# Recommendation tower: sixteen tables by one-hot matmul instead of fourteen, 64 gathers instead of 72, and one-hot rows widened from 16-bit rows

## Chip, core and metric

One core of one Trainium2 chip. The metric is the time of the whole program on the device, in microseconds (us), median of the runs shown.

## What is computed

512 samples each pick one row of 128 numbers from each of 32 tables (11 tables of 1,000 rows, 12 of 1,250, eight of 12,500, one of 125,000). Every pair of the 32 picked rows is multiplied out (496 dot products per sample), and a three-layer network runs on them:

```python
e = jnp.stack([tbl_0[ids[:, 0]], tbl_1[ids[:, 1]], ..., tbl_31[ids[:, 31]]], axis=1)
dot = jnp.einsum('bnd,bmd->bnm', e, e)
z = dot[:, iu, ju]                                  # 496 pairs, iu < ju
h = jnp.concatenate([z, dense_ctx], axis=1)         # 16 more columns
h = jnp.maximum(h @ W_top1 + b_top1, 0.0)           # 512 -> 512
h = jnp.maximum(h @ W_top2 + b_top2, 0.0)           # 512 -> 256
y = h @ W_top3                                      # 256 -> 1
```

All of it is fp32.

## The kernel before

The program is written engine by engine; each engine runs its list in order, and semaphores hold the lists together. It has two stages.

**Stage 1, picks and gathers.** Rows come into `emb` (128 partitions = the 128 numbers of a row, then sample, then table) in two ways.

A *pick* serves one small table (the 14 smallest, `PICK`). The table is loaded whole, cut in `KR` chunks of 128 rows (8 chunks for 1,000 rows, 10 for 1,250). For each chunk a one-hot row block `onehot` (128 x 512: is this row the one that sample wants?) is made, and TensorE multiplies the chunk by it (L562, L564). Since fp32r keeps only part of an fp32 number, the chunk is split in `high` (a rounded copy, ScalarE, L413) and `low` (what is left, VectorE, L310), and each chunk is two matmuls of 512 columns into `two_ps`. `onehot` is a ring of 16 chunks (`HOT`), tables and their halves are held threefold. VectorE makes most one-hot chunks by comparing ids with row numbers (L327, three chunks at a time; L317, one at a time, in the first two picks). ScalarE makes `BY_ACT` chunks of each pick (34 of the 118) in two passes per chunk: `away` = |id - row| (L420), then 1 - that, cut at zero (L435). `pick_out` copies two finished picks from `two_ps` to `emb`, `pick_alone` one (the last two).

A *gather* serves the other 18 tables: GpSimd issues an indirect DMA that fetches 128 rows (L301), 72 in all, in 20 banks. Of each block of 128 samples, one bank has 2 gathers of one table each (`lone0`, `lone1`, `MORE` = 2), and four banks have 4 (`TB`), each of 32 samples x 4 tables. TensorE turns a bank (`turn`, 2 or 4 transposes into `turn_ps`), ScalarE copies it to `emb` (`emb_out`). `rows` holds four banks (`ROWS_HELD`), so the gathers of bank k wait until bank k-4 was turned. In stage 1, TensorE turns bank t-1 behind pick t.

In stage 1, ScalarE's list per pick t is: one-hot chunks of pick t+2, `pick_out` at odd t, `emb_out(t-1)`, `away` of pick t+3, `high` of pick t+3. VectorE's is: `low` of a piece, one-hot chunks, `low` of the next piece, and so on.

**Stage 2, dots and layers.** TensorE forms the dot products of 64 samples at a time (`dot_group`, 2 x 32 small matmuls, L604), in two pairs of PSUM banks by turns; ScalarE and VectorE copy one half each to `dot_sb` (`dots_out`), the four 32-row parts go to HBM and come back skewed as `pairs` (`half_out`, `half_in` on ScalarE's queue, `block_out`, `block_in` on SyncE's), and layer 1 (L623), layer 2 (L634) and layer 3 (L639) follow. TensorE's list: `dot_group` 0 to 3, turn of bank 14, `dot_group` 4 and 5, turns of banks 15 and 16, the first half of group 6, layer 1 of blocks 0 and 1, turns of banks 17 and 18, and so on to the last bank, which is turned and multiplied in two halves among layer 1 of block 2.

Of the kernel before, what the change touches and what calls it, by code (L numbers as in the profile page):

```python
# [4 lines left out]
P = 128  # L5
# [5 lines left out]
PICK = 14  # L11
# [24 lines left out]
BY_ACT = [2, 1, 2, 2, 2, 2, 2, 2, 3, 2, 2, 4, 4, 4]  # L36
# [34 lines left out]
def build(nc, row_ids, pick_ids, tables, lone0, lone1, picked, context, w1, w2, small, y):  # L71
# [4 lines left out]
    with ctx:  # L76
# [9 lines left out]
        lone = [lone0, lone1]  # L86
        ident = sb("ident", [P, P], f32)
        id_sb = sb("id_sb", [P, 2, TILE0[NB]], i32)
        row_no = sb("row_no", [P, TILE0[NB]], i32)
# [4 lines left out]
        own_row = sb("own_row", [P, KR[0]], f32)  # L94
        less_row = sb("less_row", [P, len(STEPS), KRMAX], f32)
# [7 lines left out]
        away = sb("away", [P, AWAY, B], mybir.dt.float16)  # L103
# [48 lines left out]
        less_row_ready = sem("less_row_ready")  # L152
# [4 lines left out]
        away_ready = sem("away_ready")  # L157
# [68 lines left out]
        def _(sp):  # L226
            def ids_load(t):
                if t >= IDS_HELD:
                    sp.wait_ge(onehot_dve, by_dve(t - IDS_HELD + 1))
                    sp.wait_ge(away_ready, ACT0[t - IDS_HELD + 1])  # L230
                sp.dma_start(pick_id[:, t % IDS_HELD, :], pick_ids[:, t, :]).then_inc(pick_ids_in[t], 16)
# [53 lines left out]
        def _(pool):  # L285
# [6 lines left out]
            pool.wait_ge(row_ids_in, 16)  # L292
            for k in range(NB):
                if k == 1:
                    pool.wait_ge(row_no_ready, 1)
                if k >= ROWS_HELD:
                    pool.wait_ge(turned, k - ROWS_HELD + 1)
                for i in range(TILES[k]):
                    c = TILE0[k] + i
                    one_table = k % BANKS == 0  # L300
                    pool.indirect_dma_start(  # L301
                        rows[:, k % ROWS_HELD, i, :], None, lone[i] if one_table else tables,
                        bass.IndirectOffsetOnAxis(ap=id_sb[:, 0, c:c + 1] if one_table else row_no[:, c:c + 1], axis=0)
# [3 lines left out]
        def _(dve):  # L307
# [5 lines left out]
            def make_onehots(t, k0, k1):  # L313

                i, k = STEPS.index(KR[t]), k0
                while t < ALONE and k < k1:
                    dve.tensor_scalar(onehot[:, CHUNK0[t] + k, :], pick_id[:, t, :], own_row[:, k:k + 1], None,  # L317
                                      ALU.is_equal).then_inc(onehot_dve, 1)
                    k += 1
                while k < k1:  # L320
# [7 lines left out]
                    k += n  # L328

# [12 lines left out]
            dve.tensor_copy(own_row[:, :], own_row_i[:, 0, 0:KR[0]]).then_inc(own_row_ready, 1)  # L342
            dve.wait_ge(row_ids_in, 16)
            dve.tensor_tensor(row_no[:, :], id_sb[:, 0, :], id_sb[:, 1, :].bitcast(f32), ALU.add).then_inc(row_no_ready, 1)
            dve.wait_ge(own_row_ready, len(STEPS) + 1)
            for i, k in enumerate(STEPS):
                dve.tensor_scalar(less_row[:, i, 0:k], own_ps[:, i, 0:k], -1.0, None, ALU.mult).then_inc(less_row_ready, 1)
# [53 lines left out]
        def _(act):  # L401
# [371 lines left out]
```

## Time and profile before

| | |
|---|---|
| median of 3 runs | 121.43 us (121.08 to 122.03) |
| span of the profiled execution | 149.4 us |
| TensorE matmul busy | 118.9 us (80%) |
| VectorE busy | 76.3 us (51%) |
| ScalarE busy | 79.4 us (53%) |
| GpSimd busy | 72.0 us (48%) |
| mean granted TensorE clock | 0.931 |
| HBM read, written | 17.02 MB, 2.13 MB |

The profiled execution is 28 us longer than the median run. Busy time is the sum of an engine's instructions; shares are of the span and mix both stages. Times in the trace count from the span's start.

### The profile page before, as it was taken

How to read it: one execution, taken by the hardware profiler on the slowest of the kernel's cores; microseconds unless marked ns; L12 is line 12 of the kernel's file. 1: busy time of each engine (PE TensorE's matmuls, PEld its weight loads, DVE VectorE, ACT ScalarE, POOL GpSimd, SP SyncE). 2: the span in 40 equal slices, each digit the busy share in tenths (PEclk: the TensorE clock that was granted, in tenths of full speed). 3: DMA queues.
4: the chain of work that ended last, by engine and by line, in shares of the span. 5: the costliest groups of instructions: out<-in, count | busy, mean ns of one | idle time of the engine just before them, and what ended most of it. 6: DMA issues, size and time to landing. Idle time of an engine off the chain costs nothing.

```text
span 149.4 us, 2614 instructions
## 1 busy us (share of the span) xinstructions
PE 118.9 (80%) x1008; PEld 95.5 (64%) x1008; DVE 76.3 (51%) x106; ACT 79.4 (53%) x128; POOL 72.0 (48%) x80
## 2 busy tenths in 40 slices
PE   0689993599996998798799931289829899999994
PEld 0568871268773875486566721289729788998972
DVE  2999961199969996984969000013103033123411
ACT  3699674199939969999999300030512112210022
POOL 3787777278747747747747777300550720000000
PEclk9999999569999999999999996559986999999999
DMA  4798763136763587379511121102471731015000
GB/s 136 248 335 306 234 207 97 35 61 212 225 205 81 190 263 239 72 241 311 170 35 47 50 55 50 47 0 72 136 222 35 202 77 41 7 35 171 9 0 1
DMA packets 10990, 19.29 MB, mean 129 GB/s; under 512 B 2385, under 2 KB 7377, under 8 KB 10978
## 3 DMA queue, kind: packets, MB, share of 16 engines
q1 hardware_dynamic: 7234, 12.96, 27.9%
q0 software_dynamic: 2304, 4.72, 11.7%
q10 hardware_dynamic: 1440, 1.44, 2.8%
q8 instruction: 8, 0.13, 0.4%
q14 instruction: 4, 0.03, 0.1%
HBM read 17.02 MB, written 2.13 MB: 128 GB/s over the span
## 4 chain that ended last, share of the span: by engine, by line
PE 66%; issue 15%; DVE 11%; ACT 4%; DMA 2%; DVEq 1%; SPq 0%
PE two_ps L562 16%; PE two_ps L564 14%; DVE onehot L327 8%; PE free_ps L604 8%; PE two_ps L623 8%; PE two_ps L604 7%; PE turn_ps L572 4%; DVE low L310 3%; PE free_ps L634 3%; PE two_ps L634 2%; ACT emb L403 2%; DMA home<-picked 2%; PE two_ps L639 1%; PE turn_ps L623 1%; DVEq L364 1%
## 5 line engine op out<-in xcount | busy, mean ns | idle before, releaser
L301 POOL DMA_INDIRECT rows<-tables,row_no x64 | 63.4, 991 | 39.4 <-issue 18.0
L562 PE MATMUL two_ps<-onehot,high 128*128 128x512 f32 x118 | 50.9, 432 | 12.6 <-DVE low L310 5.2
L564 PE MATMUL two_ps<-onehot,low 128*128 128x512 f32 x118 | 48.2, 408 | 1.3 <-issue 1.3
L327 DVE TENSOR_TENSOR onehot<-pick_id,free_ps 128x1536 fp32r<-128x1536 int16 (+2 forms) x25 | 41.5, 1662 | 6.4 <-remote 5.2
L562 PEld LDWEIGHTS two_ps<-onehot,high 128*128 128x128 f32 x118 | 23.4, 198 | 23.7 <-issue 15.1
L564 PEld LDWEIGHTS two_ps<-onehot,low 128*128 128x128 f32 x118 | 23.6, 200 | 5.5 <-issue 1.5
L310 DVE TENSOR_TENSOR low<-home,high 128x512 fp32r<-128x512 f32 (+1 forms) x33 | 20.8, 631 | 8.6 <-issue 6.3
L420 ACT ACTIVATE away<-pick_id,less_row 128x512 f16<-128x512 int16 x34 | 22.3, 712 | 0.0
L604 PE MATMUL free_ps<-emb 128*64 128x64 f32 x272 | 12.7, 231 | 11.8 <-issue 10.5
L435 ACT ACTIVATE onehot<-away 128x512 fp32r<-128x512 f16 x34 | 19.2, 622 | 2.0 <-remote 1.9
L604 PEld LDWEIGHTS free_ps<-emb 128*64 128x64 f32 x272 | 10.7, 140 | 14.0 <-issue 11.9
L403 ACT ACTIVATE emb<-turn_ps 128x512 f32<-128x512 f32 (+1 forms) x20 | 10.8, 545 | 15.3 <-PE turn_ps L572 6.9
L403 ACT ACTIVATE high<-home 128x1024 fp32r<-128x1024 f32 (+2 forms) x17 | 15.9, 937 | 2.0 <-DMA home<-picked 2.0
L192 DVE COPY home<-free_ps 128x512 f32<-128x512 f32 x4 | 2.8, 692 | 24.3 <-PE free_ps L604 24.3
L403 ACT ACTIVATE home<-free_ps 128x512 f32<-128x512 f32 (+1 forms) x5 | 2.8, 554 | 22.6 <-remote 19.7
L623 PE MATMUL two_ps<-pairs,w_sb 128*128 128x128 f32 x104 | 12.9, 278 | 0.3 <-issue 0.3
L623 PEld LDWEIGHTS two_ps<-pairs,w_sb 128*128 128x128 f32 x104 | 12.1, 192 | 0.7 <-issue 0.5
L403 ACT ACTIVATE emb<-two_ps 128x1024 f32<-128x1024 f32 (+1 forms) x8 | 8.9, 1117 | 6.2 <-PE two_ps L564 6.2
L572 PE MATMUL turn_ps<-ident,rows 128*128 128x128 f32 x68 | 11.0, 283 | 1.4 <-issue 1.4
L604 PE MATMUL two_ps<-emb 128*64 128x64 f32 x240 | 10.9, 265 | 1.1 <-issue 1.1
L301 POOL DMA_INDIRECT rows<-lone,id_sb x8 | 7.7, 968 | 8.1 <-remote 2.9
L331 DVE TENSOR_SCALAR h<-two_ps,small_sb 128x128 f32<-128x128 f32 x15 | 4.3, 345 | 13.8 <-PE two_ps L623 12.9
(38 smaller groups left out, 63.2 us busy)
## 6 DMA issues: line engine op xcount, KB each, us to landing
home<-picked SPq DMA_DIRECT2D x10, 512.0 KB
home<-picked SPq DMA_DIRECT2D x3, 640.0 KB
pick_id<-pick_ids SPq DMA_DIRECT2D x12, 128.0 KB
w_sb<-w SPq DMA_DIRECT2D x3, 512.0 KB
dot_out<-home SPq DMA_DIRECT2D x10, 128.0 KB, 2.3
rows<-tables,row_no POOLq DMA_INDIRECT x64
dot_out<-home ACTq DMA_DIRECT2D x6, 128.0 KB, 2.5
pairs<-dot_out SPq DMA_DIRECT2D x10, 64.0 KB, 2.0
```

What stands on the lines that cost most here:

```text
L301: pool.indirect_dma_start(rows[:, k % ROWS_HELD, i, :], None, lone[i] if one_table else tables, bass.IndirectOffsetOnAxis(ap=id_sb[:, 0, c ...
L310: dve.tensor_tensor(low[:, at, a:b], table[:, at, a:b], high[:, at, a:b], ALU.subtract).then_inc(low_ready, 1)
L327: dve.tensor_tensor(onehot[:, c % HOT:c % HOT + n, :], ids, own, ALU.is_equal).then_inc(onehot_dve, n)
L403: return act.activation(out, in_, ACT.Copy)
L420: act.activation(away[:, m % AWAY, :], pick_id[:, t % IDS_HELD, :], ACT.Abs, bias=less_row[:, i, k:k + 1]).then_inc(away_ready, 1)
L435: act.activation(onehot[:, c % HOT, :], away[:, m % AWAY, :], ACT.Relu, bias=1.0, scale=-1.0).then_inc(onehot_act, 1)
L562: pe.matmul(out, high[:, at, D * k:D * (k + 1)], onehot[:, c % HOT, :], start=(k == 0), stop=False)
L564: pe.matmul(out, low[:, at, D * k:D * (k + 1)], onehot[:, c % HOT, :], start=False, stop=(k == KR[t] - 1)).then_inc(picked_done, 1)
L572: last = pe.transpose(turn_ps[k % 2][:, i * P:(i + 1) * P], rows[:, k % ROWS_HELD, i, :], ident[:, :])
L604: last = pe.matmul(out, e, e, start=True, stop=True, tile_position=(0, 64 * h))
L623: last = pe.matmul(h1_ps[r][n], w1_sb[:, c, n * P:(n + 1) * P], pairs[:, r:r + 1, :, c, :], start=(c == 0), stop=(c == PC - 1))
L634: return pe.matmul(h2_ps[part][n], w2_sb[:, c, n * P:(n + 1) * P], h1[:, c, samples(part)], start=(c == 0), stop=(c == N1 - 1))
```

## The change

- `PICK` 14 to 16: two tables of 1,250 rows more are picked, 138 chunks instead of 118. The order of the first fourteen picks stays.
- The gathers lose the two `lone` tables: 64 gathers, 16 equal banks of four, all of 32 samples x 4 tables.
- `LAG` = 3: TensorE turns bank t-3 behind pick t (before: bank t-1), and ScalarE's `emb_out` follows with the same lag. Banks 0 to 12 are turned in stage 1, so `dot_group` 0 to 5 run without a turn between them; banks 13, 14 and 15 are turned where 17, 18 and 19 were.
- ScalarE's `away` passes are gone, and its one-hot chunks (`BY_ACT`, now 81 of the 138) are made in two steps on two engines: VectorE compares 16-bit ids with the row number and writes a 16-bit row (`make_narrow`, one instruction per chunk, into `narrow`, two picks held), and ScalarE copies all chunks of a pick to `onehot` at once, 16 bits to fp32r (one instruction, two where the ring wraps).
- VectorE's own one-hot chunks go from 84 to 57. `make_narrow(t+1)` stands ahead of the `low` pieces of pick t.

```diff
-PICK = 14
+PICK = 16
-BY_ACT = [2, 1, 2, 2, 2, 2, 2, 2, 3, 2, 2, 4, 4, 4]
+BY_ACT = [2, 4, 5, 5, 5, 5, 5, 5, 5, 5, 5, 6, 6, 6, 6, 6]
-MORE = GF - 4 * TB
-BANKS = 1 + BLK // SUB
+BANKS = BLK // SUB
-TURNED = PICK - 1
-TABLES_HELD, IDS_HELD, HOT, AWAY, ROWS_HELD = 3, 4, 16, 8, 4
+LAG = 3
+TABLES_HELD, IDS_HELD, HOT, ROWS_HELD = 3, 4, 16, 4
...
+            def make_narrow(t):
+
+                i = STEPS.index(KR[t])
+                if t >= 2:
+                    dve.wait_ge(onehot_act, ACT0[t - 1])
+                for n in range(BY_ACT[t]):
+                    k = ACT_K0[t] + n
+                    dve.tensor_scalar(narrow[:, t % 2, n, :], pick_id[:, t % IDS_HELD, :], own_row[:, i, k:k + 1], None,
+                                      ALU.is_equal).then_inc(narrow_ready, 1)
...
             for j in range(PIECES0):
                 make_onehots(0, PIECE * j, min(PIECE * (j + 1), KR[0] - BY_ACT[0]))
+                if j == 1:
+                    make_narrow(0)
                 if j == PIECES0 - 1:
                     dve.wait_ge(pick_ids_in[1], 16)
+                    make_narrow(1)
                     make_onehots(1, DVE_K0[1], DVE_K0[1] + AHEAD)
...
             for t in range(1, PICK):
+                if t + 1 < PICK:
+                    dve.wait_ge(pick_ids_in[t + 1], 16)
+                    make_narrow(t + 1)
                 dve.wait_ge(pick_ids_in[t], 16)
...
             def make_onehots(t):
 
-                for m in range(ACT0[t], ACT0[t + 1]):
-                    c = CHUNK0[t] + ACT_K0[t] - ACT0[t] + m
-                    act.wait_ge(away_ready, m + 1)
-                    if c >= HOT:
-                        act.wait_ge(picked_done, c - HOT + 1)
-                    act.activation(onehot[:, c % HOT, :], away[:, m % AWAY, :], ACT.Relu, bias=1.0, scale=-1.0
-                                   ).then_inc(onehot_act, 1)
+                act.wait_ge(narrow_ready, ACT0[t + 1])
+                c0, n0 = CHUNK0[t] + ACT_K0[t], 0
+                while n0 < BY_ACT[t]:
+                    at = (c0 + n0) % HOT
+                    n = min(BY_ACT[t] - n0, HOT - at)
+                    if c0 + n0 + n > HOT:
+                        act.wait_ge(picked_done, c0 + n0 + n - HOT)
+                    act.activation(onehot[:, at:at + n, :], narrow[:, t % 2, n0:n0 + n, :], ACT.Copy).then_inc(onehot_act, n)
+                    n0 += n
...
-                if t:
-                    emb_out(t - 1)
+                if t >= LAG:
+                    emb_out(t - LAG)
                 if t + 3 < PICK:
-                    make_away(t + 3)
                     split_high(t + 3)
...
             for t in range(PICK):
                 pick(t)
-                if t:
-                    turn(t - 1)
-            turn(TURNED)
+                if t >= LAG:
+                    turn(t - LAG)
             pe.wait_ge(pick_emb_ready, TWOS + 1)
-            dot_group(0)
-            dot_group(1)
-            dot_group(2)
-            dot_group(3)
-            for k in range(TURNED + 1, NB - 5):
-                turn(k)
-            dot_group(4)
-            dot_group(5)
-            turn(NB - 5)
-            turn(NB - 4)
+            for grp in range(GROUPS - 2):
+                dot_group(grp)
             dot(6, 0)
             pe.wait_ge(weights_in, 64)
             layer1(0)
```

VectorE's list at the start of stage 1, from the third piece of pick 0 (its one-hot chunks) to the first `low` piece of pick 2. Before:

```order
L317 TENSOR_SCALAR onehot<-pick_id,own_row 128x512 x2
L310 TENSOR_TENSOR low<-home,high 128x256
L317 TENSOR_SCALAR onehot<-pick_id,own_row 128x512 x3
L310 TENSOR_TENSOR low<-home,high 128x512
L317 TENSOR_SCALAR onehot<-pick_id,own_row 128x512 x2
L310 TENSOR_TENSOR low<-home,high 128x512 x2
```

And of the change, the same place and the whole list of pick 2 behind it:

```order
L330 TENSOR_SCALAR narrow<-pick_id,own_row 128x512 x4
L310 TENSOR_SCALAR onehot<-pick_id,own_row 128x512 x2
L303 TENSOR_TENSOR low<-home,high 128x256
L330 TENSOR_SCALAR narrow<-pick_id,own_row 128x512 x5
L310 TENSOR_SCALAR onehot<-pick_id,own_row 128x512 x2
L303 TENSOR_TENSOR low<-home,high 128x512 x2
L330 TENSOR_SCALAR narrow<-pick_id,own_row 128x512 x5
L303 TENSOR_TENSOR low<-home,high 128x512
L320 TENSOR_TENSOR onehot<-pick_id,free_ps 128x1536
L303 TENSOR_TENSOR low<-home,high 128x512
```

The last `low` piece of pick 0 and the first of pick 1 now stand behind four and five `narrow` rows; a pick in mid-stage has five `narrow`, two `low` and one three-chunk one-hot, where it had two `low` and two three-chunk one-hots.

ScalarE's list in mid-stage, its part at pick 5 and the first row of the next (with the semaphores it waits for): one-hot chunks of pick 7, picks 4 and 5 out, a bank out, and the work on pick 8. Before:

```order
L435 ACTIVATE onehot<-away 128x512 [waits picked_done,away_ready] x2
L403 ACTIVATE emb<-two_ps 128x512x2 [waits picked_done]
L403 ACTIVATE emb<-turn_ps 128x4x32x4 [waits turned]
L420 ACTIVATE away<-pick_id,less_row 128x512 [waits onehot_act,pick_ids_in8]
L420 ACTIVATE away<-pick_id,less_row 128x512 [waits onehot_act] x2
L403 ACTIVATE high<-home 128x1024 [waits picked_done,table_in8]
L435 ACTIVATE onehot<-away 128x512 [waits picked_done,away_ready] x3
```

And of the change:

```order
L432 ACTIVATE onehot<-narrow 128x2560 [waits picked_done,narrow_ready]
L411 ACTIVATE emb<-two_ps 128x512x2 [waits picked_done]
L411 ACTIVATE emb<-turn_ps 128x4x32x4 [waits turned]
L411 ACTIVATE high<-home 128x1024 [waits picked_done,table_in8]
L432 ACTIVATE onehot<-narrow 128x2560 [waits picked_done,narrow_ready]
```

Two or three one-chunk passes of each of two kinds per pick became one wide copy of five chunks (six in the picks of ten chunks).

TensorE's list at the start of stage 2. Before:

```order
L604 MATMUL two_ps<-emb 64x64 x32
L572 MATMUL turn_ps<-ident,rows 128x128 x4
L604 MATMUL free_ps<-emb 64x64 x32
L604 MATMUL two_ps<-emb 64x64 x32
L572 MATMUL turn_ps<-ident,rows 128x128 x6
L604 MATMUL free_ps<-emb 64x64 x16
L623 MATMUL two_ps<-pairs,w_sb 128x128 x32
```

And of the change:

```order
L581 MATMUL two_ps<-emb 64x64 x32
L581 MATMUL free_ps<-emb 64x64 x32
L581 MATMUL two_ps<-emb 64x64 x32
L581 MATMUL free_ps<-emb 64x64 x16
L600 MATMUL two_ps<-pairs,w_sb 128x128 x32
```

Ten transposes left this place; the dots and layer 1 follow one another.

## Rows read from the trace of the kernel before

**Rows 1.** Core list: span and mean granted TensorE clock.

```profile
core 0: 149.4 us, clock 0.931
```

**Rows 2.** Busy time by stretch: PE, PEld, DVE, ACT, POOL, granted clock, DMA share, GB/s.

```profile
25.00:30.00 5.00, 2.63 (x7) 1.56 (x8) 0.61 (x1) 1.12 (x2) 1.81 (x3) 0.58 0.16 39
```

**Rows 3.** Chain that ended last, stage 2: start, length, what.

```profile
84.83 1.27 PE free_ps L604 x36
...
98.12 3.18 PE two_ps L604 x64
101.31 1.87 PE free_ps L604 x64
...
105.04 0.59 PE turn_ps L572 x4
...
111.64 3.40 PE two_ps L604 x63
115.04 0.82 PE turn_ps L572 x6
...
115.88 0.61 ACT emb L403
```

**Rows 4.** Timeline, 15 to 20 us: start, length, engine, instruction, idle time before it.

```profile
15.03 0.48 PE L562 MATMUL two_ps<-onehot,high 128*128 128x512 f32 x1
...
19.17 0.48 PE L562 MATMUL two_ps<-onehot,high 128*128 128x512 f32 x1
...
19.37 1.14 ACT L403 ACTIVATE emb<-two_ps 128x1024 f32<-128x1024 f32 x1 [1.93 <-PE two_ps L564]
```

**Rows 5.** Busy time over 45 to 80 us: sum and mean per 5 us.

```profile
sum 35.00, PE 30.07 PEld 21.71 DVE 29.14 ACT 33.74 POOL 23.09; mean PE 4.30 PEld 3.10 DVE 4.16 ACT 4.82 POOL 3.30
```

**Rows 6.** Timeline of ScalarE, 33 to 37 us.

```profile
33.22 1.12 ACT L403 ACTIVATE emb<-two_ps 128x1024 f32<-128x1024 f32 x1
...
34.23 0.57 ACT L403 ACTIVATE emb<-turn_ps 128x512 f32<-128x512 f32 x1
...
34.70 1.32 ACT L420 ACTIVATE away<-pick_id,less_row 128x512 f16<-128x512 int16 x2
...
35.93 1.04 ACT L403 ACTIVATE high<-home 128x1024 fp32r<-128x1024 f32 x1
...
36.88 1.13 ACT L435 ACTIVATE onehot<-away 128x512 fp32r<-128x512 f16 x2
```

**Rows 7.** Groups by shape: ScalarE's rounded copy of a 10-chunk table, VectorE's one-chunk compare.

```profile
L403 ACT ACTIVATE high<-home 128x1280 fp32r<-128x1280 f32 x3 | 3.8, 1266 | 0.0
...
L317 DVE TENSOR_SCALAR onehot<-pick_id,own_row 128x512 fp32r<-128x512 int16 x13 | 5.7, 481 | 0.0
```

**Rows 8.** Timeline of VectorE, mid-stage.

```profile
33.33 0.69 DVE L310 TENSOR_TENSOR low<-home,high 128x512 fp32r<-128x512 f32 x1
...
33.93 1.75 DVE L327 TENSOR_TENSOR onehot<-pick_id,free_ps 128x1536 fp32r<-128x1536 int16 x1
...
35.60 0.69 DVE L310 TENSOR_TENSOR low<-home,high 128x512 fp32r<-128x512 f32 x1
```

**Rows 9.** Timeline, start of stage 1: VectorE, ScalarE, GpSimd, TensorE at pick 1.

```profile
8.30 1.27 DVE L317 TENSOR_SCALAR onehot<-pick_id,own_row 128x512 fp32r<-128x512 int16 x3
...
8.69 1.05 ACT L403 ACTIVATE high<-home 128x1024 fp32r<-128x1024 f32 x1
...
8.82 1.17 POOL L301 DMA_INDIRECT rows<-tables,row_no  x1 [0.30 <-issue]
...
11.15 0.47 PE L562 MATMUL two_ps<-onehot,high 128*128 128x512 f32 x1 [0.49 <-issue]
```

**Rows 10.** GpSimd's gathers: length in ns, min/median/max, first and last start.

```profile
L301 POOL DMA_INDIRECT rows<-tables,row_no x64: 941/947/1487, 6.1 to 119.4; - x64
```

**Rows 11.** Timeline, last gathers and last pick.

```profile
83.72 1.05 ACT L403 ACTIVATE emb<-two_ps 128x512 f32<-128x512 f32 x1 [1.68 <-PE two_ps L564]
...
105.90 0.95 POOL L301 DMA_INDIRECT rows<-tables,row_no  x1 [10.77 <-PE turn_ps L572]
```

More of the change, by code:

```diff
@@ L50 @@
 TB, SUB = 4, 32
-MORE = GF - 4 * TB
-BANKS = 1 + BLK // SUB
+BANKS = BLK // SUB
 NB = BLOCKS * BANKS
-TILES = [TB if k % BANKS else MORE for k in range(NB)]
-TILE0 = [sum(TILES[:k]) for k in range(NB + 1)]
-TURNED = PICK - 1
-TABLES_HELD, IDS_HELD, HOT, AWAY, ROWS_HELD = 3, 4, 16, 8, 4
+TILES = NB * TB
+LAG = 3
+TABLES_HELD, IDS_HELD, HOT, ROWS_HELD = 3, 4, 16, 4
+NARROW = max(BY_ACT)
 CTX = 16
@@ L102, in build @@
         onehot = sb("onehot", [P, HOT, B], f32r)
-        away = sb("away", [P, AWAY, B], mybir.dt.float16)
+        narrow = sb("narrow", [P, 2, NARROW, B], mybir.dt.float16)
         dot_sb = home
@@ L156, in build @@
         onehot_dve = sem("onehot_dve")
-        away_ready = sem("away_ready")
+        narrow_ready = sem("narrow_ready")
         onehot_act = sem("onehot_act")
@@ L291, in _ @@
                                base=0, pattern=[[-1, P]], channel_multiplier=1).then_inc(ident_ready, 1)
-            pool.wait_ge(row_ids_in, 16)
+            pool.wait_ge(row_no_ready, 1)
             for k in range(NB):
-                if k == 1:
-                    pool.wait_ge(row_no_ready, 1)
                 if k >= ROWS_HELD:
                     pool.wait_ge(turned, k - ROWS_HELD + 1)
-                for i in range(TILES[k]):
-                    c = TILE0[k] + i
-                    one_table = k % BANKS == 0
+                for i in range(TB):
+                    c = TB * k + i
                     pool.indirect_dma_start(
-                        rows[:, k % ROWS_HELD, i, :], None, lone[i] if one_table else tables,
-                        bass.IndirectOffsetOnAxis(ap=id_sb[:, 0, c:c + 1] if one_table else row_no[:, c:c + 1], axis=0)
+                        rows[:, k % ROWS_HELD, i, :], None, tables,
+                        bass.IndirectOffsetOnAxis(ap=row_no[:, c:c + 1], axis=0)
                     ).then_inc(late_rows_in if k == NB - 1 and i >= TB // 2 else rows_in[k % ROWS_HELD], 16)
@@ L567, in turn @@
             def turn(k):
-                pe.wait_ge(rows_in[k % ROWS_HELD], 16 * sum(TILES[k % ROWS_HELD:k + 1:ROWS_HELD]))
+                pe.wait_ge(rows_in[k % ROWS_HELD], 16 * TB * (k // ROWS_HELD + 1))
                 if k >= 2:
                     pe.wait_ge(emb_ready, k - 1)
-                for i in range(TILES[k]):
+                for i in range(TB):
                     last = pe.transpose(turn_ps[k % 2][:, i * P:(i + 1) * P], rows[:, k % ROWS_HELD, i, :], ident[:, :])
@@ L580, in last_turn @@
                 else:
-                    pe.wait_ge(rows_in[k % ROWS_HELD], 16 * (sum(TILES[k % ROWS_HELD:k + 1:ROWS_HELD]) - TB // 2))
+                    pe.wait_ge(rows_in[k % ROWS_HELD], 16 * (TB * (k // ROWS_HELD + 1) - TB // 2))
                 pe.wait_ge(emb_ready, k - 1 + half)
@@ L588, in dot @@
             def dot(grp, j):
-                r, half = divmod(2 * grp + j, BANKS - 1)
-                pe.wait_ge(emb_ready, BANKS * r + half + 2)
+                pe.wait_ge(emb_ready, 2 * grp + j + 1)
                 if grp >= 2:
@@ L722, in by_gather @@
             of = a[BLK * r:BLK * (r + 1)]
-            tiles += [of[:, f] for f in range(4 * TB, GF)]
             tiles += [of[SUB * u:SUB * (u + 1), 4 * i:4 * i + 4].reshape(P) for u in range(BLK // SUB) for i in range(TB)]
```

56 lines of the change are left out of this document (11 added, 45 removed).

## Prediction

> **What bounds the kernel now.** I read the span first, then where it stands still, then each stage's fullest engine.
>
> The profiled execution spans 149.4 us [rows 1], the median run takes 121.43. The excess has to be understood before a sum is made. From 25 to 30 us every engine is mostly idle and TensorE's granted clock is 0.58, between its levels of 1.2 and 2.4 GHz, after its activity fell [rows 2]. In stage 2 the chain shows it by piece: a dot group (64 small matmuls) takes 1.87 us at full clock, but the first stands from 84.83 to 98.12, the second takes 3.18, the fifth stands from the end of a turn at 105.63 to 111.64, and the sixth takes 3.40 [rows 3]. These are 11.4 + 1.3 + 4.1 + 1.5 = 18.3 us over 1.87 each, with no dependence named. And in stage 1 signals from TensorE come late: TensorE has finished pick 1 and starts pick 2 at 15.03, yet ScalarE, idle for 1.93, starts its copy of picks 0 and 1 at 19.37 [rows 4]. I take both as a cost of this profiled execution, not of the median run. Without them stage 2, from the first dot at 84.83 to the end, is 149.4 - 84.8 - 18.3 = 46.3 us, and the median leaves 121.4 - 46.3 = 75.1 for stage 1.
>
> Stage 1 is ScalarE's. From 45 to 80 us it is busy 33.7 of 35 us, TensorE 30.1, VectorE 29.1 [rows 5]. Its steps, start to start: a pair of picks out 1.01, a bank out 0.47, an `away` pass 0.61 (1.23 for two), a rounded copy of 8 chunks 0.95 [rows 6], of 10 about 0.22 more by the lengths of 1.27 and 1.04 us [rows 6, 7]; a one-hot pass 0.52 (two last 1.13; like all its neighbours they overlap by 0.09). From its first 8-chunk copy at 8.69 us [rows 9] on it has 32 `away` (19.5), 32 one-hot (16.6), 13 copies (13.0), 12 banks (5.2), 6 pairs (6.1) and 2 single picks (2.0): 62.4, so 71.1 us if it never waits. The last pick adds about 3, since VectorE's and TensorE's work on it begins only when its rounded copy is there. That is 74, beside 75.1 from the other side; I take 74.5 for the first dot in a median run.
>
> TensorE alone would be there sooner. Eight chunks with their turn take 4.14 us (15.03 to 19.17) [rows 4]: 0.47 a chunk and 0.36 a turn of four. Pick 0 ends near 10.5; 110 chunks and 11 turns later it would be 10.5 + 51.8 + 3.8 = 66.1, and the last copy of a pick adds 1.3 to the first dot (it starts at 83.72, lasts 1.05, and the dot follows at 84.83 [rows 3, 11]; it waits 0.2 for the last matmul): 67.4. So TensorE waits 7.1 us in stage 1 today, and that is all the change can win there.
>
> **The change, part by part.**
>
> *TensorE's new work.* Twenty chunks at 0.47 are 9.4 us. Up to the last pick's end 48 transposes stand where 42 stood, 0.5 more. All of it is on the engine that must finish: its floor goes from 67.4 to 77.3. That is 9.9 us against 7.1 us of waits, so stage 1 grows even if every wait went. How many stay, I count forward.
>
> *ScalarE.* Per 8-chunk pick it now has one wide copy, 0.95, 0.47 and half of 1.01. No row shows a 2,560-column copy from 16 bits. Its bounds: a fixed 0.2 and the rate of the `high` rows, (1266 - 1040) ns for 256 columns, 0.88 ns a column, 2.3 to 2.4 in all; above, five one-hot passes, 2.6. I take 2.3, since `high` is also one wide copy. The pick is then 4.2 (4.5 above), with 10 chunks 5.0: level with TensorE's 4.14 and 5.08, where before it was 4.3 to 6.9.
>
> *VectorE.* It pays for this. Start to start, a `low` piece is 0.60, a three-chunk one-hot 1.67 [rows 8], a one-chunk compare to four-byte output 0.40 (three last 1.27, one 0.48) [rows 7, 9]. The 16-bit pass is in no row. Above, 0.40: as that compare. Below: 1,024 more columns lengthen a pass by 1.06 us [rows 8], 1.04 ns a column; the one-chunk compare runs at half that, 0.27 for its columns, which leaves 0.13 fixed, and that is the lower end. The two rates are one factor of two apart; the output of the new pass is half as wide, and I take one more factor, 0.13 + 0.13 = 0.27, which is also the middle of the bounds. By it an 8-chunk pick costs 5 x 0.27 + 2 x 0.60 + 1.67 = 4.2, a 10-chunk pick 6 x 0.27 + 1.53 + 1.67 + 0.60 = 5.4.
>
> The Trainium skill ("VectorE: DVE Perf Modes", the perf-mode tier table) has a one-source pass with 16-bit data on both sides in SBUF at four elements a cycle, against two for four-byte data. That agrees with the two-a-cycle rate of the compare rows and gives the same 0.27 for the new pass; at two a cycle it would be the 0.40 above, and the total that of the second rival.
>
> *The start.* VectorE has done the last `low` piece of pick 0 when its three compares begin at 8.30 [rows 9]. Ahead of it now stand 6 `narrow`, 1.6 us, and two compares as before: it ends near 9.8, pick 0 ends at 10.9 for 10.5. Five more `narrow` and two compares stand ahead of the first `low` of pick 1: 9.8 + 1.35 + 0.8 + 0.6, so TensorE starts pick 1 at 12.65 instead of 11.15 [rows 9] and ends it at 16.4. Nothing covers this; TensorE has no other work.
>
> *Forward.* Picks 2 and 3, 3.77 each, and the first turn: 24.3. Picks 4 to 10 are 7 x 4.2, level on all three engines: 53.7. Picks 11 to 15 are 5 x 5.08 less the last turn, 25.0, plus 0.3 in four of them because VectorE needs 5.4: 79.9. To the first dot 1.3: 81.2. Against 74.5 that is +6.7; I take 6.6, since the level stretch carries a little lead: 3.8 us of waits stay.
>
> *Gathers.* GpSimd needs about 1.25 us a gather (0.95 and 0.30 idle [rows 9, 10]), 5.0 a bank. Bank 4 may start when bank 0 is turned, 24.3, so bank 12 lands near 24.3 + 9 x 5.0 + 2 = 71, and it is turned at 79.9. Bank 15 lands near 86 and is needed past 100. With the lag of three, nothing waits. SyncE's queue moves one more table and its ids per pick; it is released by `low` of three picks back and `narrow`, both about a pick and a half early. Hidden.
>
> *Stage 2.* Gone are ten transposes, 0.59 + 0.82 on the chain, and the wait of 0.69 for the copy of bank 16 [rows 3]: 2.1 us. Some is given back: the first half of group 6 needs group 4's copy on ScalarE, which stands behind its stores and loads for blocks 0 and 1, about 12.1 us after the first dot, while TensorE now arrives at 11.3; and layer 1 of block 1 has its pairs at about 17. I take -1.6 (bounds -2.1 and -0.5).
>
> *Sum.* +6.6 - 1.6 = +5.0. On the profiled execution: 149.4 + 5.0 = 154.4 if it stood still as long; on the median, 121.4 + 5.0 = **126.4 us**.
>
> **The rivals.**
>
> *VectorE is dearer.* If the 16-bit pass costs 0.40, each of 75 passes after the start adds 0.13, 9.8, less the 1 us by which VectorE ends ahead, and VectorE bounds stage 1: 135. For it: the one-chunk compare is the only such row. Against: its rate halved where the bytes did. Chance 0.09.
>
> *VectorE is cheaper.* Near 0.15 to 0.2 a pass, the 0.3 waits go (1.2) and the start gains about 1.2: 124. With every wait gone the first dot is at 77.3 for 81.1: 122.6, even then slower by 1%. Chance 0.13.
>
> *ScalarE's wide copy gains nothing over five passes.* The change would then not relieve it: 0.3 a pick over 14 picks, 4, and ScalarE bounds: 130.5. Against: the overhead per instruction is in the rows. Chance 0.07.
>
> *The gathers starve.* Beside the three compares a gather lasts 1.17 for the median 0.95 [rows 9, 10]. If each bank lost the whole 1.35 us of its pick's `narrow`, it would take 6.35, bank 12 would land at 83.5, and the dots wait: about 129. At +0.2 a gather it is 5.8 a bank and still hidden. The Trainium skill ("SBUF — State Buffer", the "DVE blocks DMA" trap) says that a VectorE pass on two ports locks GpSimd out and leaves its DMA without descriptors; the trace shows a small part of that. Chance 0.05.
>
> *Faster.* The last gathers hold stage 2 today, and the change frees it. GpSimd idles 10.77 us until 105.90 for a turn [rows 11], with two of the twenty banks to come, and these must be fetched, turned and copied before the last dots; the new kernel has all banks by 86. By my count bank 19 lands about 21 us after the first dot in a median run and is wanted at 24. Only if it were over 8 us late would this outweigh +5.0: at 10 us, 118.7 with the saved wait. The profiled chain shows no such wait. Chance 0.04.
>
> **How the numbers follow.** The forecast as worked has 0.62, 124.5 to 129. The range 123.8 to 130.5 leaves out the dear pass (0.09), faster (0.04) and half of the costly copy. This kernel's measurement tells about 1% from no change. Faster by over 1% is 0.05; within 1%, 0.07, the cheap case's edge and what my reading of the profiled excess may be off; slower, 0.88.
>
> **What would show it.** A `narrow` row at 0.35 us length and 0.27 apart (0.48 and 0.40 for the first rival); the wide copy at 2.3; TensorE at pick 1 near 12.7; VectorE with hardly any idle time in stage 1, ScalarE with some; gathers landed a pick or more ahead of their turns; the first dot some 6 to 7 us later, less whatever the profiled execution stood still differently; groups 4 to 6 without a turn. It would be wrong if stage 1 in a median run were longer than 75 today, for late signals that cost every run, since the change lets more work stand ahead.

## The result and the profile after

The changed kernel takes 131.06 us (130.55 to 131.97), the kernel before, on the same chip, 121.63 (121.08 to 122.03): ratio 1.079, interval 1.075 to 1.084. It is slower, as forecast, but by 9.4 us where 5.0 was forecast, and it lies above the range, which ended at 130.5.

Some executions of the kernel before take about 150 us, with TensorE standing still for stretches, where the others take 121 to 122, for a reason that was not found; rows 1 to 11 (149.4 us) come from such a one. Below they are replaced by a profile of the same kernel at 121.06 us, the run c_before2. This is its core line, the first dot group of its chain, and its waits of TensorE (line, what it waited for, us in total, times, longest); they answer rows 1 and rows 3.

```profile
core 0: 119.3 us, clock 1.000
```

```profile
73.05 2.09 PE free_ps L604 x64
75.14 1.89 PE two_ps L604 x64
```

```profile
PE two_ps L562 <- DVE low L310: 5.0, 2, 4.8
PE free_ps L604 <- ACT emb L403: 1.3, 3, 0.8
PE two_ps L562 <- ACT onehot L435: 1.3, 1, 1.3
PE turn_ps L572 <- DMA rows<-tables,row_no: 0.9, 1, 0.9
PE two_ps L562 <- DVE onehot L327: 0.5, 2, 0.4
```

The same views of the changed kernel: its core line, the chain through stage 2 and to the end, and TensorE's waits.

```profile
core 0: 128.9 us, clock 1.000
```

```profile
84.81 2.08 PE free_ps L581 x64
86.89 1.87 PE two_ps L581 x64
88.76 1.87 PE free_ps L581 x64
...
96.22 1.12 PE free_ps L581 x32
97.35 7.34 PE two_ps L600 x64
```

```profile
PE two_ps L540 <- DVE low L303: 8.4, 7, 6.0
PE free_ps L581 <- ACT emb L411: 0.9, 2, 0.7
```

The spans differ by 9.6 us. Stage 1, to the first dot, is longer by 84.81 - 73.05 = 11.76. Stage 2 is shorter: 128.9 - 84.81 = 44.1 against 119.3 - 73.05 = 46.25, so 2.16 less; the dot groups follow each other at 1.87 with no turn in between. All the loss lies ahead of the first dot.

Pick 1, the second table, starts here before and after:

```profile
11.30 0.47 PE L562 MATMUL two_ps<-onehot,high 128*128 128x512 f32 x1 [1.26 <-ACT onehot L435]
```

```profile
13.62 0.50 PE L540 MATMUL two_ps<-onehot,high 128*128 128x512 f32 x1 [1.51 <-DVE low L303]
```

From there on VectorE is the engine that never rests. The order of engines in each row is PE, PEld, DVE (VectorE), ACT (ScalarE), POOL (GpSimd). The first row is of the kernel before (c_before2) from 20 to 60 us, where ScalarE was busy all the time; the second of the changed kernel from 45 to 80 us (answers rows 5). Then VectorE's timeline in mid-stage (answers rows 8), and the passes that make `narrow`, with their lengths in ns, min/median/max:

```profile
20.00:60.00 40.00, 38.13 (x175) 29.25 (x175) 38.20 (x36) 40.00 (x64) 30.81 (x31) 1.00 0.67 215
```

```profile
sum 35.00, PE 34.07 PEld 25.82 DVE 35.00 ACT 30.85 POOL 26.75; mean PE 34.07 PEld 25.82 DVE 35.00 ACT 30.85 POOL 26.75
```

```profile
31.61 1.67 DVE L330 TENSOR_SCALAR narrow<-pick_id,own_row 128x512 f16<-128x512 int16 x5
33.20 0.67 DVE L303 TENSOR_TENSOR low<-home,high 128x512 fp32r<-128x512 f32 x1
33.79 1.74 DVE L320 TENSOR_TENSOR onehot<-pick_id,free_ps 128x1536 fp32r<-128x1536 int16 x1
35.45 0.68 DVE L303 TENSOR_TENSOR low<-home,high 128x512 fp32r<-128x512 f32 x1
36.06 1.53 DVE L330 TENSOR_SCALAR narrow<-pick_id,own_row 128x512 f16<-128x512 int16 x5
37.51 0.73 DVE L303 TENSOR_TENSOR low<-home,high 128x512 fp32r<-128x512 f32 x1
```

```profile
L330 DVE TENSOR_SCALAR narrow<-pick_id,own_row x81: 332/341/550, 6.6 to 72.4; 128x512 f16<-128x512 int16 x81
```

Five `narrow` take 1.59 us from start to start of the next kind (31.61 to 33.20) and 1.45 in the next pick (36.06 to 37.51), 0.32 and 0.29 each. VectorE is busy in 35.00 of 35 us; ScalarE, the fullest engine before, has room (30.85 of 35).

The passes are not evenly apart. Of the 70 that start after 14 us, 52 are 0.255 to 0.268 us from the start of the next instruction, and 18 are 0.33 to 0.47. A gather of GpSimd ends during each of those 18, and during only one of the 52. Here are a gather that ends at 37.22, a pass that is over before that, and the next, during which it ends:

```profile
36.24 0.98 POOL L294 DMA_INDIRECT rows<-tables,row_no  x1 [0.30 <-issue]
36.58 0.34 DVE L330 TENSOR_SCALAR narrow<-pick_id,own_row 128x512 f16<-128x512 int16 x1
36.84 0.49 DVE L330 TENSOR_SCALAR narrow<-pick_id,own_row 128x512 f16<-128x512 int16 x1
```

The wide copy and the gathers, which answer rows 7 and rows 10:

```profile
L432 ACT ACTIVATE onehot<-narrow 128x2560 fp32r<-128x2560 f16 x9 | 21.1, 2343 | 1.7 <-DVE narrow L330 1.3 <-PE two_ps L542 0.4
```

```profile
L294 POOL DMA_INDIRECT rows<-tables,row_no x64: 940/945/2137, 3.6 to 88.3; - x64
```

### The profile page after: what moved, and what is told of

It is laid out like the page before. It is cut to its first block, busy times and chain, and to the rows that moved or that the text cites. A ratio compares the mean times of both kernels' runs of the same rounds, so it can differ in the third digit from the quotient of the medians.

```text
span 128.9 us, 2689 instructions
## 1 busy us (share of the span) xinstructions
PE 117.2 (91%) x1040; PEld 95.9 (74%) x1040; DVE 88.3 (68%) x184; ACT 79.6 (62%) x76; POOL 67.2 (52%) x72
## 4 chain that ended last, share of the span: by engine, by line
PE 37%; DVE 8%; ACT 8%; issue 5%; DMA 4%; ACTq 0%; SPq 0%; DVEq 0%
PE two_ps L600 8%; PE free_ps L581 7%; PE two_ps L581 6%; PE two_ps L540 5%; PE two_ps L542 5%; DVE onehot L320 4%; ACT emb L411 3%; DMA dot_out<-home 3%; DVE low L303 2%; ACT high L411 2%; DMA pairs<-dot_out 2%; DVE narrow L330 2%; PE two_ps L616 2%; PE turn_ps L600 2%; ACT onehot L432 2%
## 5 line engine op out<-in xcount | busy, mean ns | idle before, releaser
L540 PE MATMUL two_ps<-onehot,high 128*128 128x512 f32 x138 | 57.8, 419 | 8.6 <-DVE low L303 8.4
L542 PE MATMUL two_ps<-onehot,low 128*128 128x512 f32 x138 | 55.0, 399 | 0.0
L540 PEld LDWEIGHTS two_ps<-onehot,high 128*128 128x128 f32 x138 | 26.5, 192 | 20.2 <-DVE low L303 8.8
L432 ACT ACTIVATE onehot<-narrow 128x2560 fp32r<-128x2560 f16 (+3 forms) x17 | 38.0, 2243 | 4.8 <-DVE narrow L330 2.6
L542 PEld LDWEIGHTS two_ps<-onehot,low 128*128 128x128 f32 x138 | 26.7, 193 | 4.8
L320 DVE TENSOR_TENSOR onehot<-pick_id,free_ps 128x1536 fp32r<-128x1536 int16 (+2 forms) x20 | 27.8, 1394 | 0.0
L303 DVE TENSOR_TENSOR low<-home,high 128x512 fp32r<-128x512 f32 (+1 forms) x39 | 24.3, 626 | 1.2 <-ACT high L411 1.2
L330 DVE TENSOR_SCALAR narrow<-pick_id,own_row 128x512 f16<-128x512 int16 x81 | 25.1, 372 | 0.0
L581 PE MATMUL free_ps<-emb 128*64 128x64 f32 x272 | 9.1, 223 | 0.9 <-ACT emb L411 0.9
L550 PEld LDWEIGHTS turn_ps<-ident,rows 128*128 128x128 f32 x60 | 7.4, 140 | 1.7
```

Source lines behind the costliest of these rows:

```text
L303: dve.tensor_tensor(low[:, at, a:b], table[:, at, a:b], high[:, at, a:b], ALU.subtract).then_inc(low_ready, 1)
L320: dve.tensor_tensor(onehot[:, c % HOT:c % HOT + n, :], ids, own, ALU.is_equal).then_inc(onehot_dve, n)
L330: dve.tensor_scalar(narrow[:, t % 2, n, :], pick_id[:, t % IDS_HELD, :], own_row[:, i, k:k + 1], None, ALU.is_equal).then_inc(narrow_ready, 1)
L432: act.activation(onehot[:, at:at + n, :], narrow[:, t % 2, n0:n0 + n, :], ACT.Copy).then_inc(onehot_act, n)
L540: pe.matmul(out, high[:, at, D * k:D * (k + 1)], onehot[:, c % HOT, :], start=(k == 0), stop=False)
L542: pe.matmul(out, low[:, at, D * k:D * (k + 1)], onehot[:, c % HOT, :], start=False, stop=(k == KR[t] - 1)).then_inc(picked_done, 1)
```

## The experiments

Times are medians; ratios are to the kernel before, run beside each, with 95% intervals in brackets. Differences to the changed kernel are of medians that were not taken beside each other. Code is shown in part; `...` stands for lines left out.

**The kernel before again (c_before, c_before2).**

> The kernel before once more, for a profile that does not stand still. The profile of the changed kernel spans 128.9 us where its run took 130.7, so 1.8 us lie outside the span; the span here should be 121.6 - 1.8 = 119.8. If my split of the excess was right, the first dot is at 74.5 minus those 1.8, near 73, and 46.3 us follow. If instead stage 2 took the same 44.1 + 2.1 as the changed kernel's, the first dot is near 73.6. A first dot near 77 would mean that the late signals of the first profile cost every run.

> The kernel before again. In the first four runs the kernel before took 150.6 us, as its first profile did (149.4 us span), and stood still at the same places, while the runs compared with the change took 121.6. So the standing still belongs to the chip, not to the profile. Here I expect either 150 again or, on a chip without it, a span of 119.8 with the first dot near 73.5.

c_before took 152.8 us, the kernel before 150.6 beside it without a profile; c_before2 took 121.06, with 122.03 beside it. The first shows where such an execution stands still, TensorE's waits for nothing that the profile names:

```profile
PE free_ps L604 <- issue: 10.0, 13, 1.8
...
PE two_ps L562 <- issue: 4.1, 8, 1.0
PE two_ps L564 <- issue: 2.7, 3, 1.6
```

So the excess of rows 1 to 3 is neither the kernel's nor the profiler's. Nor does it belong to one chip, as the second expectation has it: the chip of c_before2 took 150.4 us for the same kernel later. In c_before2 stage 1 ends at 73.05, close to the 73 and the 73.5 that were expected.

**The new way to make one-hot rows, at fourteen tables (narrow14, narrow14b).** The kernel before with `narrow` and the wide copy in place of `away` and its pass, and with the rows dealt as in the change:

```
-BY_ACT = [2, 1, 2, 2, 2, 2, 2, 2, 3, 2, 2, 4, 4, 4]
+BY_ACT = [2, 4, 5, 5, 5, 5, 5, 5, 5, 5, 5, 6, 6, 6]
```

> The kernel before with only the one-hot scheme of the change (VectorE's 16-bit rows, ScalarE's wide copies, BY_ACT 2, 4, 5 x9, 6 x3); 14 tables, 72 gathers and the turns as before. If VectorE bounds stage 1 with this scheme (it was busy 5.0 of 5 us in the changed kernel), the first dot is two picks of 5.5 us ahead of the changed kernel's 84.8, near 73.7, and the time is within 1.5 us of before. If TensorE's added chunks alone made the change slow and the scheme frees 3 us of waits as I forecast, the time is 118 to 119.

> The kernel before with only the one-hot scheme of the change. VectorE bounds it: first dot near 73.7, the time within 1.5 us of before. TensorE bounds it and the scheme frees 3 us of waits: 3 us less than before (118 to 119 on a chip that takes 121.6).

narrow14b took 121.38 us, 0.996 [0.992, 1.001], first dot at 72.78; narrow14, beside a kernel before of 150.6 us, 150.42, 1.005 [1.000, 1.011]. Alone the new way is worth nothing that can be measured, because VectorE takes ScalarE's place as the full engine (the same stretch as in c_before2 above):

```profile
20.00:60.00 40.00, 39.42 (x182) 30.32 (x182) 40.00 (x75) 39.19 (x32) 30.86 (x31) 1.00 0.66 210
```

**Sixteen tables, rows made the old way (away16, away16b).** The changed kernel with `away` back:

```
-BY_ACT = [2, 4, 5, 5, 5, 5, 5, 5, 5, 5, 5, 6, 6, 6, 6, 6]
+BY_ACT = [2, 1, 2, 2, 2, 2, 2, 2, 3, 2, 2, 4, 4, 4, 4, 4]
```

> The changed kernel with the old one-hot scheme back (away and one-hot passes on ScalarE, 2 chunks a pick and 4 in each ten-chunk pick); sixteen tables, 64 gathers and the lag of three stay. If ScalarE bounds it as before, two picks of 6.9 us are added and 2 us of stage 2 saved: near 133. If the scheme of the change is the dearer one, this is below 131.

> The changed kernel with the old one-hot scheme (16 tables, 64 gathers, lag of three). ScalarE bounds it as before: two picks of 6.9 us more and 2 us less in stage 2, near 133. If the new scheme is the dearer one, below 131.

away16b took 132.53 us, 1.087 [1.078, 1.096], first dot at 86.59, ScalarE busy in all of 20 to 80 us. So the tables and turns bring the loss. By the ratios the new rows take back about 1 us of it, but the two intervals overlap (the changed kernel's is 1.075 to 1.084). Where the kernel before takes 150.6 us, the same kernel (away16) was faster than it: 143.66 us, 0.960 [0.951, 0.970].

**The 16-bit passes left out (stale16, stale16b).** From pick 3 on VectorE makes no `narrow`, and ScalarE copies pick 2's rows again, so these picks fetch other rows, with the same work for ScalarE and TensorE. 69 passes are gone (the expectations say 68), and with them VectorE's wait for ScalarE's copies:

```
-                if t >= 2:
-                    dve.wait_ge(onehot_act, ACT0[t - 1])
-                for n in range(BY_ACT[t]):
+                for n in range((BY_ACT[t] if t < 2 else NARROW) if t < 3 else 0):
...
-                act.wait_ge(narrow_ready, ACT0[t + 1])
+                act.wait_ge(narrow_ready, (ACT0[t + 1] if t < 2 else ACT0[2] + NARROW))
```

> The changed kernel without VectorE's 16-bit passes from pick 3 on (ScalarE copies the rows of pick 2 again, so 13 picks are of wrong rows; 68 passes are left out). If VectorE bounds stage 1, TensorE's own floor of 77.3 plus the 2 us of the start and the 1 us by which the first piece came late appear: first dot near 80.5, total near 126.5. If TensorE already bounds it, the time stays near 131.

> The changed kernel without VectorE's 16-bit passes from pick 3 on (68 passes left out, ScalarE copies the rows of pick 2 again). VectorE bounds the change: first dot near 80.5, total near 126.5. TensorE already bounds it: near 131.

stale16b took 127.26 us, 1.044 [1.034, 1.055]: 3.8 us below the changed kernel. TensorE then has no wait inside stage 1 once pick 1 has begun, VectorE is busy in 42.9 of the 60 us from 20 to 80, and the kernel is still 4.4% slower. (stale16, beside a kernel before of 150.6 us: 144.18, 0.964.)

**A pass more in each pick (spare16).** One further 16-bit compare in picks 3 to 15, 13 in all (`out` is memory that nobody reads by then):

```
...
+                if t >= 3:
+                    dve.tensor_scalar(out, pick_id[:, t % IDS_HELD, :], own_row[:, i, 0:1], None, ALU.is_equal)
```

> The changed kernel with one further 16-bit compare pass of VectorE in each of picks 3 to 15 (13 passes, results written to memory that nobody reads until layer 1's data arrive). Theory A (VectorE's stream sets stage 1): each pass adds its start-to-start distance 0.29 to 0.33, together +3.8 to +4.3 us, device time about 135. Theory B (VectorE has slack in the picks of ten chunks, or TensorE binds): +0 to +2 us.

134.13 us, 1.103 [1.095, 1.110]: 3.1 more, 0.24 a pass, and the first dot 2.86 later. VectorE's stream sets stage 1. The expectation's 3.8 was too high: it took the mean distance of 0.29 to 0.33, while most passes here too are 0.263 apart, and nearly all of that is passed on.

**The passes of pick 2 later (start16).**

```
-                if t + 1 < PICK:
+                if 1 < t < PICK - 1:
...
+                if t == 1:      # behind pick 1's low pieces and rows
+                    make_narrow(2)
```

> The changed kernel with VectorE's six or five 16-bit rows of pick 2 made behind pick 1's low pieces and rows, not ahead of them. Theory A (pick 1 starts late because these passes stand ahead of its first low piece): pick 1 starts about 1.5 us earlier than 13.62 and every pick after it too, device time 129.5 to 130. Theory B (VectorE's sum over the picks binds from the first pick on, order does not matter): first picks earlier, the gain eaten by pick 5 or so, device time 130.8 to 131.3.

130.86 us, 1.078 [1.069, 1.087]: no gain. Pick 1 starts at 12.38 instead of 13.62, and the first dot at 84.19, 0.6 earlier. Some 0.4 of the head start is no merit of the edit: ScalarE's first `high` began at 4.58 for 4.98. Half of it is spent again by the first turn (24.44 against 25.00), as theory B has it: order on a full engine moves the wait, and hardly the end.

**One-chunk compares at sixteen tables (ts16).** VectorE's own one-hot rows by a scalar column, as in the first two picks:

```
...
-                    dve.tensor_tensor(onehot[:, c % HOT:c % HOT + n, :], ids, own, ALU.is_equal).then_inc(onehot_dve, n)
+                    dve.tensor_scalar(onehot[:, c % HOT, :], pick_id[:, t % IDS_HELD, :], own_row[:, i, k:k + 1], None,
+                                      ALU.is_equal).then_inc(onehot_dve, 1)
```

> The changed kernel with one edit: VectorE's one-hot rows of a pick are made by compares of one chunk each (a scalar column of row numbers, as the first two picks have them, 128x512, about 0.41 us apart) in place of one compare of three chunks (128x1536, 1.74 us, 1.67 apart). Same rows, same work elsewhere. Theory A (VectorE's own stream, 4.37 us a pick, sets picks 4 to 10, since the 16-bit passes are 0.29 to 0.33 apart): VectorE's stream falls by 3 x (0.557 - 0.41) = 0.44 us a pick to 3.93, below TensorE's 4.12 with a turn, picks 4 to 10 come at 4.12 or so apart (about -0.2 x 10 and some more in the picks of ten chunks), the first dot at about 82, device time 127.5 to 129. Theory B (two more tables cost what TensorE's own dots and turns cost and VectorE only follows): no more than 0.5 us, device time 130.5 to 131.

127.45 us, 1.046 [1.038, 1.053], the same as stale16b without its 16-bit passes. Its VectorE in mid-stage, and all engines from 20 to 80 us (PE, PEld, DVE, ACT, POOL, granted clock):

```profile
39.48 1.27 DVE L317 TENSOR_SCALAR onehot<-pick_id,own_row 128x512 fp32r<-128x512 int16 x3
40.66 0.68 DVE L303 TENSOR_TENSOR low<-home,high 128x512 fp32r<-128x512 f32 x1
```

```profile
20.00:80.00 60.00, 60.00 (x289) 49.63 (x288) 52.51 (x135) 56.08 (x46) 44.07 (x44) 1.00 0.61 202
```

Three rows in 1.18 instead of 1.66 us. TensorE is busy in all of the 60 us, with turns 4.10 apart (5.0 in ten-chunk picks), as in stale16b. From pick 1 on this is TensorE's floor, and no relief of VectorE or ScalarE goes below it. Of the 5.6 us that are left over before, some lie ahead of it: pick 1 starts at 13.96, 2.7 later than in c_before2. The profiled executions of ts16 and stale16b also lost about 1.2 us to a lower clock (last section); three further executions of each, with a mean granted clock of 1.00, took 126.6 to 127.8.

**The same compares at fourteen tables (ts14).** The kernel before with that edit and its rows dealt anew:

```
-BY_ACT = [2, 1, 2, 2, 2, 2, 2, 2, 3, 2, 2, 4, 4, 4]
+BY_ACT = [2, 1, 1, 2, 1, 2, 1, 2, 1, 2, 1, 2, 2, 2]
```

> The kernel before (fourteen tables, two passes of ScalarE for its rows) with VectorE's compares of three chunks replaced by single compares of one chunk each, and the rows dealt anew: ScalarE makes 1 or 2 a pick (list 2,1,1,2,1,2,1,2,1,2,1,2,2,2) in place of 2 to 4. By the durations VectorE then has 6.5 x 0.41 + 2 x 0.64 = 3.95 us a pick where it has 4.5, ScalarE about 3.8 where it has 4.4, and TensorE's 4.12 (ten-chunk picks 5.0) binds. Theory A (the two engines that make the rows bind the kernel before): first dot from 73.05 to about 69.5, device time 117.5 to 119. Theory B (the gathers, 1.25 us apart on GpSimd until 96, bind the last turns and so the end): first dot earlier, but the end moves by less than half of that, device time 119.5 to 121.

129.99 us, 1.065 [1.057, 1.074]: above both theories. B named the right engine, but both had the first dot earlier, and it came 9.5 later, at 82.56. VectorE and ScalarE have less to do; TensorE waits for gathered rows. Its profile is of an execution of 132.21 us, the longest of five. TensorE's wait for rows, the gathers, and three gathers in a row with VectorE beside them:

```profile
PE turn_ps L571 <- DMA rows<-tables,row_no: 12.7, 6, 3.6
```

```profile
L301 POOL DMA_INDIRECT rows<-tables,row_no x64: 940/947/2281, 6.2 to 106.4; - x64
```

```profile
27.57 1.49 POOL L301 DMA_INDIRECT rows<-tables,row_no  x1 [0.30 <-issue]
29.36 1.49 POOL L301 DMA_INDIRECT rows<-tables,row_no  x1 [0.31 <-issue]
31.16 2.28 POOL L301 DMA_INDIRECT rows<-tables,row_no  x1 [0.30 <-issue]
```

```profile
28.07 1.27 DVE L324 TENSOR_SCALAR onehot<-pick_id,own_row 128x512 fp32r<-128x512 int16 x3
29.26 0.68 DVE L310 TENSOR_TENSOR low<-home,high 128x512 fp32r<-128x512 f32 x1
29.86 1.67 DVE L324 TENSOR_SCALAR onehot<-pick_id,own_row 128x512 fp32r<-128x512 int16 x4
31.44 0.68 DVE L310 TENSOR_TENSOR low<-home,high 128x512 fp32r<-128x512 f32 x1
```

These three last 1.49, 1.49 and 2.28 us for the median 0.947. In all, 27 of the 64 last over 1.1 us, where 10 do in c_before2. The last one is issued at 106.4 against 96.2 in c_before2 (below), 10.2 later, and the span is 130.0 for 119.3, 10.7 longer.

```profile
L301 POOL DMA_INDIRECT rows<-tables,row_no x64: 940/944/1496, 6.2 to 96.2; - x64
```

The Trainium skill ("SBUF — State Buffer", the "DVE blocks DMA" trap) says that a VectorE pass in a mode that takes two ports locks GpSimd out of the pair, so that it can't write its descriptors. This run agrees, with 1.49 and 2.28 us for 0.947. But such compares do not always lengthen gathers: in ts16, with three of them a pick for ts14's six or seven and `narrow` besides, the mean gather is 1.021 us, no longer than the changed kernel's 1.037. What makes the difference was not tested.

**Dealing or compares? (deal14, deal14b, deal14c)** The list of ts14 with the three-chunk compares kept.

> The kernel before with the list of rows for ScalarE of the run ts14 (2,1,1,2,1,2,1,2,1,2,1,2,2,2) and VectorE's three-chunk compares as they were. VectorE has 7 x 0.557 + 2 x 0.61 = 5.1 us in a pick where ScalarE makes one row and 4.5 where it makes two. Theory A (ts14 was slow because one-chunk compares lengthen the gathers, 1.145 us on average and up to 2.28, and the turns wait for them): here the gathers keep 0.945 to 1.0 us and the last is issued at 96 to 97, TensorE never waits for a gather by more than 1 us in stage 1, and the time is set by VectorE: first dot at 77 to 79, device time 124.5 to 127. Theory B (the dealing of rows was the fault, the compares not): gathers lengthen here too and the time is 129 to 131.

The three took 150.33, 150.21 and 150.66 us beside 149.89, 150.41 and 150.26 for the kernel before, so their times can't be set beside ts14's, whose kernel before took 121.9. The gathers' lengths can be read all the same, since the kernel before has them alike in both (mean 1.003 and 1.006 us):

```profile
L301 POOL DMA_INDIRECT rows<-tables,row_no x64: 942/947/1494, 6.3 to 118.1; - x64
```

Their mean is 1006 ns (985 and 1008 in the other two), against ts14's 1145. So the dealing alone does not lengthen the gathers; with the one-chunk compares in place of the others they are longer. What deal14 takes beside a kernel before of 122 us stays open, and so does what share of ts14's 8 us the gathers have.

**Everything relieved at sixteen tables (combo16, combo16b, combo16c).** ts16 with start16's order and one `narrow` less a pick.

> The changed kernel with three edits: VectorE's rows by one-chunk compares in place of the three-chunk compare, its 16-bit rows of pick 2 behind pick 1's low pieces and rows, and one 16-bit row fewer a pick for ScalarE to copy (list 2,4,4,4,4,4,4,4,4,4,4,5,5,5,5,5). By the measured distances VectorE then has 4 x 0.41 + 2 x 0.62 + 4 x 0.30 = 4.1 us a pick, ScalarE about 0.95 + 1.9 + 1.05 = 3.9, TensorE 4.10. Theory A (with one-chunk compares TensorE binds from pick 1 on, and what is left over the kernel before is two tables of TensorE's time): pick 1 starts at about 12.4 instead of 13.96, the first dot comes at 79.5 to 80.5, device time 125 to 126.5, still slower than the kernel before. Theory B (more one-chunk compares lengthen the gathers, as they do with fourteen tables, and a turn comes to wait for one): 127 to 129.

Here too the kernel before took 149.9 to 150.4 us beside them: 144.25, 144.58 and 146.15 us, 0.961 [0.954, 0.969] and 0.965 [0.955, 0.976] of before in the first two. In combo16 the first four turns come 4.14, 4.10 and 4.10 apart (24.18, 28.32, 32.42, 36.52), the same distance as in ts16 though ScalarE copies a chunk less a pick, so it is TensorE's. Neither theory is settled: what combo16 takes beside a kernel before of 122 us was not measured.

## Why the prediction was wrong

**The kernel before: the step failed by 1.45 us.** The text took stage 2 from a span and subtracted it from the median device time: 121.4 - 46.3 = 75.1, then 74.5. About 1.8 us of every run lie outside the span (121.06 for a span of 119.3, 130.72 for 128.9). 119.3 - 46.25 gives the measured 73.05. ScalarE's forward count of 74 agreed with the wrong figure, so the agreement proved nothing. That the excess of the profile was no part of the median run, and stage 2 of 46.3, were right (46.25).

**"Waits go from 7.1 to 3.8": wrong.** The counted floors were 67.4 and 77.3. The time above them was 73.05 - 67.4 = 5.65 before and 84.81 - 77.3 = 7.5 after: it rose. Of the 11.76 us, 9.9 are the two tables as counted, 1.9 are more waiting. The rise lies at the start, where pick 1 begins 2.3 later (1.5 forecast). From pick 1 to the first dot the time above the floor is 4.9 before and 4.4 after, where the forecast had 6.5 and 1.8: the change was to free mid-stage and hardly did. That the floors were counted well is shown by stale16b and ts16, where TensorE never waits after pick 1 has begun: 67.7 us from there to the first dot, 66.5 without the lower clock, for 66.8 counted. In place of 81.2 the first dot stands at 84.81, 3.6 later, and the places are:

- *The start, +1.06.* Pick 1 was to begin at 12.65 and begins at 13.62, and the first turn was to end at 24.3 and ends near 25.36. VectorE waited for a first `high`, which ScalarE began at 4.98, against 3.86 in c_before2, because the first piece of the table landed later, though issued at the same 1.22. In the eleven profiles of kernels with sixteen tables TensorE starts pick 0 at 5.4 to 6.2, in the nine with fourteen at 4.8 to 5.4. Why it lands later was not found.
- *Picks 4 to 10, +1.5.* 30.9 us where 29.4 were forecast. The five passes take 1.45 to 1.59 with what follows, not 1.35. The term of 0.27 is right for a pass by itself: at the start four take 1.06 (8.60 to 9.66), and in mid-stage most are 0.263 apart. What the sum put at nothing is the pass during which a gather ends, 0.33 to 0.47: one or two in each pick, on the engine that had no room, 2.5 us over 0.263 in all. The text asked what VectorE does to the gathers, and not what they do to it. (That the gather's end is the cause is argued from 18 cases in 18, and 13 in 15 in ts16; no run took the gathers away.) And pick 10 makes six passes, for pick 11, where the sum has five: it takes 4.61.
- *Picks 11 to 15, +1.05.* Turns are 5.6 to 5.7 apart, forecast 5.4, for the same reason with six passes.

Together 3.6, and with 1.45 of before 5.1, which is 11.76 for the forecast 6.7. That stage 1 before was ScalarE's is right (40.00 of 40 us busy in c_before2). But the text called the new mid-stage "level on all three engines"; it was VectorE's alone. stale16b (-3.8 by the medians), ts16 (-3.6, likewise) and spare16 (+3.1) show this from both sides; start16 shows that the order at the start carried little.

**Stage 2: -1.6 forecast, -2.16 measured**, at the favourable bound of -2.1. Nothing was given back: the first half of group 6 starts at 96.22, right behind group 5 (94.36 + 1.87), and layer 1 runs through at 7.34 for both blocks.

**ScalarE: right.** The wide copy at 2.3 measured 2.343, and ScalarE has room. The third rival did not come.

**The gathers: the forecast of the changed kernel right, the view of before too easy.** In the changed kernel GpSimd waits 0.3 us for a turn and nobody waits for it. Single gathers reach 2.14 us beside `narrow`, but with 64 instead of 72 there is room: 8 x 1.25 = 10 us. In c_before2 GpSimd goes from one gather to the next without a wait, 1.3 apart on average, until 96.2; a turn waits 0.9 for it at 55.35, and the last gathered bank is turned at 100.48. So the gathers were near to being a second limit of the kernel before: the chain that ended last runs through them up to that turn, and the last gather on it took 4.95 us to land. ts14 eased the first limit and lengthened the gathers in one edit, so how far the kernel would go with gathers of their old length is not shown. The "Faster" rival was right that the change frees GpSimd; but in c_before2 its last bank was in time, so freeing it paid only in stage 2.

**The rivals on VectorE.** By the length of a pass (341 ns; 350 was expected, 480 in the first rival) the forecast stands: the pass has the rate that the text gave it, and the Trainium skill ("VectorE: DVE Perf Modes", the tier table) agrees by this row. What differs is the mean distance, 0.299 from 14 us on, by the passes that meet the end of a gather. 131.06 lies outside the range and between the forecast and the first rival, whose condition (a pass at 0.40) did not hold.

## What to carry to other kernels

Count each engine's stream per period and look at the margin, not at the likeliest value: where three engines are within 0.1 us of each other, every term's error on the fullest adds up over the periods and none cancels. Before a total is split, subtract span from span and not span from device time. And before an engine's passes are made faster or more, look at what runs beside them, in both directions: here the `narrow` passes were lengthened where a gather ended, and VectorE's one-chunk compares came with 3.6 us less at sixteen tables, where the gathers stayed as long as they were, and with 8 more at fourteen, where they grew.

## What the runs showed of the hardware

- A 128x512 compare of VectorE from 16 to 16 bits lasts 0.341 us and is 0.263 from start to start of the next, and 0.33 to 0.47 where a GpSimd gather ends during it (18 of 18 in the changed kernel).
- Beside VectorE's one-chunk compares (16 bits to fp32r) in ts14 a gather of 0.947 us lasts up to 2.28, 1.145 in the mean; beside its three-chunk compares, which read row numbers from PSUM (`free_ps`), 1.003 to 1.006.
- In the profiles of ts16 and stale16b the granted clock falls to 0.75 and 0.70 from 15 to 20 us, with 2.5 and 3 us of these at its lower level (0.50 of full speed, 1.2 GHz), after TensorE stood idle for 1.8 us ahead of pick 1; the changed kernel, idle for 1.5 there, kept 1.00. This is ts16's row (PE, PEld, DVE, ACT, POOL, clock):

```profile
15.00:20.00 5.00, 5.00 (x18) 3.99 (x17) 5.00 (x15) 2.73 (x2) 3.78 (x5) 0.75 0.62 203
```

TensorE gets through 18 matmuls there where the changed kernel has 24, and from pick 1 to the first turn ts16 takes 12.62 us where the changed kernel takes 11.38.
